# A Mamba block with an fp8 FFN: root, chunk load, tile copy and one low part moved in the first stage

## The chip, the cores and the metric

The kernel runs on 1 core of one Trainium2 chip. The metric is the device time of one execution in microseconds (us); the median of 3 runs before the change is 1058.67.

## The reference

Four sequences of 512 positions with 512 features; DI = 1024 channels, N = 16 states, 4 taps, R = 128.

```python
xn = layernorm(x)
proj = einsum('blh,eh->bel', xn, Win); hs, gate = proj[:, :DI], proj[:, DI:]
hs = silu(causal_conv4(hs) + bconv)
dt_in, Bm, Cm = split(einsum('bdl,pd->blp', hs, Wx))
dt = softplus(einsum('blr,dr->bld', dt_in, Wdt) + bdt)
h = exp(A * dt) * h + dt * Bm * hs          # scan over l, for every channel and state
y = (sum_n h * Cm + hs * D) * silu(gate)
ffn = dot8(gelu(dot8(xn, w0)) * dot8(xn, w1), w_linear)      # operands in fp8 e4m3
out = x + y @ Wout.T + ffn
```

## The kernel before

There are two stages, one after the other, written out by hand for each engine. **Stage A** (`stage_a`) makes for each of the 4 batches everything that the scan needs and leaves it in DRAM; **stage B** (`stage_b`) runs the scan, the gate, the FFN and the output projection for 32 units (4 batches by 8 channel tiles of 128). Each engine executes its instructions in the order written; semaphores tie them. On SP and TensorE the first three batches are one loop, on the others they are written out.

Stage A for batch b, with k the channel tile (8 of them), h one of the 4 feature tiles:

- TensorE (`tensor_a`) projects tile k in 12 matmuls of 512 columns (`project`; each product is split into a high and a low part of both operands, L625 to L627), and from k = 3 on adds `ssm_inputs(k - 3)` after it: five matmuls of hs_hi and hs_lo, the first, from hs_lo, written to dt_ps at L625 ("low product"). At the batch's end come low products 5, 6, 7 with the transposes of the next batch's xn between them, then eight `project_dt` (L673), one for each k, beside the four parts of the next batch's projection 0, then its projection 1.
- ScalarE (`scalar_a`): `newest_tap(b, k)` (L550) starts the convolution of tile k from PSUM, `silu` (L563) ends it, `high_part` (L568) rounds it. `deviation(b + 1)` (L525) is the square root for the next batch's layernorm; it needs a table load of its own, and one to come back (L584). `copy_tiles` (L514, L515) copies a transposed tile of the next batch out of PSUM, the fourth after the load of the table for Exp and Ln (L599). Then eight times Exp and Ln (L604, L606), with the next batch's tap 0 between units 5 and 6.
- VectorE (`vector_a`): three steps of convolution a tile (`convolve`, L445, 128x512 each), at k = 3 the layernorm's `scales` (L410 to L416), at k = 1, 4, 7 the cast of a 1 MB chunk of FFN weights to fp8 (L473), at the end the `statistics` for batch b + 2 (L399 to L405, in batches 0 and 1), then bc (L489), and for each k the sum with its cap (L483) and dt (L495).
- POOL (`gpsimd_a`): the low part hs_lo = hs - hs_hi of each tile (L362), two tiles of the next batch's xn (L367), the four low parts of its transposed tiles (L373), and dt times hs for each k (L378, "du"). In the last batch `head_start` (L858) stands before the du: the first three dbu products of stage B, 128x1024 each.
- SP (`sync_a`) issues all DMAs from one queue: the xnT store (L299), at k = 0, 3, 6 a cast chunk's store and the next chunk's load (L287, L262), a store of each hs (L307), of each dt and du together (L322, four slots: dt of tile k waits for the store of tile k - 4), and in the last batch loads for stage B (L311, L317).

```python
                if not last:
                    for h in range(HT):
                        pool.wait_ge(xnT_ready, (b + 1) * HT + h + 1 + 2)
                        nc.gpsimd.tensor_tensor(xnT_lo[:, h, :], xnT[:, h, :], xnT_hi[:, h, :], ALU.subtract).then_inc(lo_ready, 1)
```

## Time and profile before

| | us |
|---|---|
| median of 3 runs (lowest, highest) | 1058.67 (1058.31, 1058.89) |
| profiled execution, its own time | 1060.56 |
| its span | 1058.8 |
| busy: TensorE, VectorE, ScalarE, POOL | 910.5, 994.5, 832.8, 913.0 |

| stretch, us | TensorE busy | VectorE | ScalarE | POOL | granted clock | DMA share |
|---|---|---|---|---|---|---|
| 26 to 70 (batch 0) | 38.65 | 35.51 | 38.22 | 28.09 | 0.96 | 0.72 |
| 70 to 116 (batch 1) | 41.73 | 38.89 | 38.83 | 30.44 | 1.00 | 0.80 |
| 116 to 161 (batch 2) | 41.62 | 34.41 | 39.10 | 30.38 | 1.00 | 0.81 |
| 161 to 205 (batch 3) | 34.96 | 32.59 | 30.47 | 27.89 | 1.00 | 0.95 |
| 205 to 1058 (stage B) | 739.44 | 836.50 | 671.47 | 785.98 | 0.95 | 0.31 |

The page gives the span and each engine's busy time in it; the second table is the view of busy time by stretch of time. Batch boundaries are those of ScalarE's first silu table. A timeline row gives start and duration of one instruction and, in brackets, how long its engine stood idle before it and what ended that. Times of the trace lie within one execution; its own time is 1.76 us above the span, and 1.9 us above the median of the runs.

### The profile page before, as it was taken

The numbers are of one execution on the slowest core, as the hardware profiler recorded it, in microseconds if no ns is written. First come the engines' busy times: TensorE is split into PE (matmuls) and PEld (weight loads), VectorE is DVE, ScalarE is ACT, GpSimd is POOL, SyncE is SP. The second block draws the span as 40 slices with busy tenths as digits, with TensorE's granted clock in tenths as the row PEclk, the third lists the DMA queues.
The fourth block names the chain that finished last, engine by engine and source line by source line (L and its number), as shares of the span: only waits on it lengthen the run. The fifth ranks groups of instructions, "written<-read, shape, count | busy, mean of one in ns | idle before, by whom it ended". The sixth has DMA issues, their size and how long they took to land.

```text
span 1058.8 us, 14443 instructions
## 1 busy us (share of the span) xinstructions
PE 910.5 (86%) x4328; PEld 561.2 (53%) x4328; DVE 994.5 (94%) x1190; ACT 832.8 (79%) x1164; POOL 913.0 (86%) x512
## 2 busy tenths in 40 slices
PE   5888989577789987998799879887998798879998
PEld 4656757244445554554455556554555455445554
DVE  6887878799999999999999999999999999999996
ACT  5888987688888666898896668988866689888662
POOL 4566674899999899899999998999899989998993
PEclk9999999889889998999999979998999899999999
DMA  8678879991112129232121292221213922212101
GB/s 305 219 264 281 302 264 345 377 334 55 61 41 90 40 75 332 107 103 80 60 90 41 97 346 88 86 80 60 90 41 115 350 78 75 80 59 81 41 1 40
DMA packets 53208, 150.26 MB, mean 142 GB/s; under 512 B 5776, under 2 KB 14096, under 8 KB 50064
## 3 DMA queue, kind: packets, MB, share of 16 engines
q1 hardware_dynamic: 53136, 149.41, 40.6%
q8 instruction: 32, 0.52, 0.2%
q14 instruction: 40, 0.33, 0.1%
HBM read 111.37 MB, written 38.01 MB: 141 GB/s over the span
## 4 chain that ended last, share of the span: by engine, by line
DVE 32%; issue 25%; POOL 17%; ACT 11%; PE 7%; DMA 6%; SPq 1%; DVEq 1%; POOLq 0%; ACTq 0%
POOL dbu L858 11%; DVE da L1125 11%; DVE prod L1100 8%; DVE hp L1125 6%; POOL hp L1088 4%; DMA wf<-in_wffn 3%; ACT da L1019 2%; DVE conv L445 2%; PE yT L1251 2%; ACT L1008 1%; ACT L1007 1%; DVE gate_bf L1138 1%; DVE y L1108 1%; PE mm L1200 1%; DMA b_all<-bc_d 1%
## 5 line engine op out<-in xcount | busy, mean ns | idle before, releaser
L1019 ACT ACTIVATE da<-unit,neg_a 128x512 f32<-128x512 f32 x512 | 338.6, 684 | 156.9 <-DVE prod L1100 154.0
L858 POOL TENSOR_TENSOR dbu<-unit,b_head 128x1024 f32<-128x1024 f32 x192 | 450.0, 2367 | 0.0
L1125 DVE TENSOR_TENSOR_SCAN da<-da,dbu 128x512 f32<-128x512 f32 x352 | 417.9, 1218 | 1.3
L1251 PE MATMUL yT<-ident,prod 128*128 128x128 f32 x1408 | 227.7, 291 | 93.0 <-DVE prod L1100 92.2
L1251 PEld LDWEIGHTS yT<-ident,prod 128*128 128x128 f32 x1408 | 168.2, 147 | 227.7 <-DVE prod L1100 188.2
L1088 POOL TENSOR_TENSOR hp<-hp,c_head 128x512 f32<-128x512 f32 x128 | 162.7, 1271 | 50.7 <-DVE gate_bf L1141 46.1
L1125 DVE TENSOR_TENSOR_SCAN hp<-da,dbu 128x512 f32<-128x512 f32 x160 | 193.5, 1210 | 3.3 <-ACT da L1019 3.3
L1100 DVE TENSOR_TENSOR prod<-da,c_head 128x512 f32<-128x512 f32 x256 | 171.7, 671 | 0.0
L1200 PE MATMUL mm<-xn_b,w_sb 128*128 128x512 fp8e4 x512 | 143.8, 414 | 15.9 <-ACT acc L1039 12.9
L858 POOL TENSOR_TENSOR dbu<-unit,b_all 128x1024 f32<-128x1024 f32 x64 | 151.0, 2359 | 0.0
L1212 PE MATMUL mm<-xnT_b,wgate 128*128 128x512 f32 x256 | 128.8, 601 | 0.0
L1160 PE MATMUL mm<-y,wout_sb 128*128 128x512 f32 x242 | 114.6, 593 | 0.8 <-DVE y L1108 0.8
L1251 PE MATMUL yT<-ident,hp 128*128 128x128 f32 x640 | 98.9, 278 | 0.0
L1200 PEld LDWEIGHTS mm<-xn_b,w_sb 128*128 128x128 fp8e4 x512 | 51.5, 105 | 66.0 <-issue 34.7
L362 POOL TENSOR_TENSOR hs_lo<-hs,hs_hi 128x512 fp32r<-128x512 f32 x32 | 41.8, 1307 | 44.8 <-ACT hs_hi L568 44.8
L445 DVE SCALAR_TENSOR_TENSOR conv<-proj,cols_sb,conv 128x511 f32<-128x511 f32 (+2 forms) x96 | 71.0, 746 | 8.7 <-ACT conv L550 6.3
L1251 PEld LDWEIGHTS yT<-ident,hp 128*128 128x128 f32 x640 | 77.6, 145 | 0.0
L1160 PEld LDWEIGHTS mm<-y,wout_sb 128*128 128x128 f32 x242 | 43.4, 190 | 43.0 <-issue 41.9
L1100 DVE TENSOR_TENSOR prod<-da,c_all 128x512 f32<-128x512 f32 x96 | 65.0, 678 | 0.0
L1221 PE MATMUL mm<-act,w_sb 128*128 128x512 fp8e4 x256 | 61.8, 379 | 0.0
L625 PE MATMUL proj<-xnT_lo,win_hi 128*128 128x512 f32 x128 | 57.0, 446 | 0.2 <-DVE conv L445 0.2
L378 POOL TENSOR_TENSOR dt_du<-dt_du,hs 128x512 f32<-128x512 f32 x32 | 40.9, 1283 | 13.0 <-DVE dt_du L495 12.4
(123 smaller groups left out, 1285.8 us busy)
## 6 DMA issues: line engine op xcount, KB each, us to landing
unit<-unit_d SPq DMA_DIRECT2D x32, 768.0 KB, 4.2
unit_d<-dt_du SPq DMA_DIRECT2D x32, 512.0 KB, 2.9
wf<-in_wffn SPq DMA_DIRECT2D x12, 1024.0 KB, 7.1
c_head<-bc_d SPq DMA_DIRECT2D x24, 512.0 KB, 4.1
b_head<-bc_d SPq DMA_DIRECT2D x18, 512.0 KB, 4.9
unit_d<-hs SPq DMA_DIRECT2D x32, 256.0 KB, 6.6
w_sb<-w_d SPq DMA_DIRECT2D x64, 128.0 KB, 3.8
wgate<-in_win_gate SPq DMA_DIRECT2D x32, 256.0 KB, 2.7
```

The lines of the kernel that those rows point to most:

```text
L445: ins = nc.vector.scalar_tensor_tensor(out=conv[:, k % 2, back:L], in0=proj[k % 3][:, 0:L - back], scalar=cols_sb[:, k, C_TAP + TAPS - 1 - ...
L625: nc.tensor.matmul(bank, hi, low, start=start, stop=False)
L858: return nc.gpsimd.tensor_tensor(dbu[:, n % DBUS:n % DBUS + NS, :], twice, b_all[n // NS], ALU.mult)
L1019: nc.scalar.activation(da[n % SLOTS][:, :], unit[:, k % 2, 0, :], ACT.Exp, scale=neg_a[:, k, n:n + 1]).then_inc(da_ready, 1)
L1088: nc.gpsimd.tensor_tensor(tile, tile, c_all[m // NS][:, m % NS, :], ALU.mult).then_inc(hp_ready, 1)
L1100: nc.vector.tensor_tensor(prod[:, slot, :], da[n % SLOTS][:, :], c_all[n // NS][:, n % NS, :], ALU.mult).then_inc(prod_ready, 1)
L1125: nc.vector.tensor_tensor_scan(state, da[n % SLOTS][:, :], dbu[:, n % DBUS, :], 0.0, ALU.mult, ALU.add).then_inc(scanned, 1)
L1160: return nc.tensor.matmul(bank[:, :], wout_sb[:, c, h * P:(h + 1) * P], y2[:, c, :], start=(c == first), stop=(c == last))
L1200: ins = nc.tensor.matmul(bank[:, :], wffn[:, k % 2, j, f, s, :].bitcast(FP8), xn8[:, f, :].bitcast(FP8), start=(f == 0), stop=(f == HT - 1))
L1212: ins = nc.tensor.matmul(bank[:, :], wgate[:, k % 2, c * P:(c + 1) * P], xnT[:, c, :], start=(c == 0), stop=(c == 3))
L1221: ins = nc.tensor.matmul(bank[:, :], wlin[:, i, h * P:(h + 1) * P].bitcast(FP8), act8[:, i, :].bitcast(FP8), start=(i == 0), stop=(i == HI ...
L1251: ins = nc.tensor.matmul(yT[k % 2][:, t * P:(t + 1) * P], product[:, t * P:(t + 1) * P], ident[:, :], start=False, stop=last, is_transpose ...
```

## The change

Four steps, all in stage A.

- SP: the chunk's store and the next chunk's load at k = 0 are issued before the xnT store instead of after it, in every batch.
- ScalarE: the square root for the next batch moves from after two tiles to the top of the batch, behind tap 1; of the silu table's two loads in a batch one is left. In the last batch, without a root, tap 1 now stands ahead of the table load.
- ScalarE and POOL: the copy of the next batch's fourth tile moves behind the first two Exp and Ln, its low part on POOL behind the first two du.
- VectorE and POOL: in batches 2 and 3 hs_lo of k = 7 is made by VectorE, behind its last convolution and ahead of the third cast, and no longer by POOL.

```diff
--- before.py
+++ after.py
@@ -295,11 +295,12 @@
                         wait(dt_du_stored[i], 16 * (B - 1) * (KU // DTS) + 16)
                     wait(win_split, KU)
                     wait(xn_used, B)
-                wait(xnT_ready, b * HT + HT + 2)
-                sp.dma_start(row(xnT_d, b), xnT[:, :, :].rearrange("p k l -> p (k l)")).then_inc(xnT_stored, 16)
                 for k in range(KU):
                     if k % 3 == 0:
                         chunk(k // 3)
+                    if k == 0:
+                        wait(xnT_ready, b * HT + HT + 2)
+                        sp.dma_start(row(xnT_d, b), xnT[:, :, :].rearrange("p k l -> p (k l)")).then_inc(xnT_stored, 16)
                     if k == KU - 1:
                         wait(xn8_ready, b + 1)
                         sp.dma_start(row(xn8_d, b), xn8[:, :, :].rearrange("p k l -> p (k l)")).then_inc(xn8_stored, 16)
@@ -357,6 +358,8 @@
 
             def body(b, last):
                 for k in range(KU):
+                    if k == KU - 1 and b >= B - 2:
+                        continue
                     pool.wait_ge(hs_hi_ready, b * KU + k + 1)
                     pool.wait_ge(ssm_summed, b * KU + k + 1)
                     nc.gpsimd.tensor_tensor(hs_lo[:, k % 2, :], hs[:, k, :], hs_hi[:, k % 2, :], ALU.subtract).then_inc(hs_lo_ready, 1)
@@ -367,15 +370,20 @@
                             ins = nc.gpsimd.tensor_scalar(xn[:, t, :], x_rest[:, b * LT + t, :], moments[:, t, 0:1], rstd[:, t:t + 1],
                                                           ALU.subtract, ALU.mult)
                         ins.then_inc(xn_ready, 1)
+                def low_tile(h):
+                    pool.wait_ge(xnT_ready, (b + 1) * HT + h + 1 + 2)
+                    nc.gpsimd.tensor_tensor(xnT_lo[:, h, :], xnT[:, h, :], xnT_hi[:, h, :], ALU.subtract).then_inc(lo_ready, 1)
+
                 if not last:
-                    for h in range(HT):
-                        pool.wait_ge(xnT_ready, (b + 1) * HT + h + 1 + 2)
-                        nc.gpsimd.tensor_tensor(xnT_lo[:, h, :], xnT[:, h, :], xnT_hi[:, h, :], ALU.subtract).then_inc(lo_ready, 1)
+                    for h in range(HT - 1):
+                        low_tile(h)
                 if last:
                     head_start(pool)
                 for k in range(KU):
                     pool.wait_ge(dt_ready, b * KU + k + 1 + KU)
                     nc.gpsimd.tensor_tensor(dt_du[:, k % DTS, 1, :], dt_du[:, k % DTS, 0, :], hs[:, k, :], ALU.mult).then_inc(du_ready, 1)
+                    if k == 1 and not last:
+                        low_tile(HT - 1)
 
             for b in range(B):
                 body(b, b == B - 1)
@@ -462,6 +470,11 @@
                 for k in range(KU):
                     if k > 0:
                         convolve(b, k)
+                    if k == KU - 1 and b >= B - 2:
+                        dve.wait_ge(hs_hi_ready, b * KU + k + 1)
+                        dve.wait_ge(ssm_summed, b * KU + k + 1)
+                        dve.wait_ge(hs_lo_ready, b * KU + k)
+                        nc.vector.tensor_tensor(hs_lo[:, k % 2, :], hs[:, k, :], hs_hi[:, k % 2, :], ALU.subtract).then_inc(hs_lo_ready, 1)
                     if k == 3 and not last:
                         scales(b + 1)
                     if k in (1, 4, 7):
@@ -567,9 +580,13 @@
                     act.wait_ge(ssm_summed, b * KU + k + 1)
                     nc.scalar.activation(hs_hi[:, k % 2, :], hs[:, k, :], ACT.Copy).then_inc(hs_hi_ready, 1)
 
+                newest_tap(b, 1)
+                if not last:
+                    deviation(b + 1)
                 nc.scalar.preload_act_table_set("silu_and_others")
                 for k in range(1, KU):
-                    newest_tap(b, k)
+                    if k > 1:
+                        newest_tap(b, k)
                     if k == 5 and not last:
                         act.wait_ge(scales_ready, b + 2)
                         act.wait_ge(xn_used, b + 1)
@@ -579,9 +596,6 @@
                         ins.then_inc(xn_ready, 1)
                     silu(k - 1)
                     high_part(k - 1)
-                    if k == 2 and not last:
-                        deviation(b + 1)
-                        nc.scalar.preload_act_table_set("silu_and_others")
                     if k == 4:
                         fp8_copy(b)
 
@@ -597,9 +611,9 @@
                 nc.scalar.activation(dtin[:, :], dt_ps[:, :], ACT.Copy).then_inc(dtin_copied, 1)
                 nc.scalar.activation(bc_low[:, :], bc_ps[2 * N:4 * N, :], ACT.Copy).then_inc(bc_low_copied, 1)
                 nc.scalar.preload_act_table_set("natural_log_exp_and_others")
-                if not last:
-                    copy_tiles(b + 1, HT - 1, HT)
                 for k in range(KU):
+                    if k == 2 and not last:
+                        copy_tiles(b + 1, HT - 1, HT)
                     act.wait_ge(z_ready, b * KU + k + 1)
                     nc.scalar.activation(soft[:, k % 3, :], soft[:, k % 3, :], ACT.Exp).then_inc(exp_done, 1)
                     act.wait_ge(exp_done, b * KU + k + 1)
```

ScalarE at the head of batch 0, as the programs order it (sd<-vare is the root, conv<-proj a tap, hs<-conv a silu, hs_hi<-hs the copy behind it). Before:

```order
L532 ACTIVATE win_hi<-win_rest 128x512 x2
L570 ACT_TABLE_LOAD
L550 ACTIVATE conv<-proj,cols_sb 128x512
L563 ACTIVATE hs<-conv 128x512
L568 ACTIVATE hs_hi<-hs 128x512
L550 ACTIVATE conv<-proj,cols_sb 128x512
L563 ACTIVATE hs<-conv 128x512
L568 ACTIVATE hs_hi<-hs 128x512
L525 ACT_TABLE_LOAD
L525 ACTIVATE sd<-vare 128x4
L584 ACT_TABLE_LOAD
L550 ACTIVATE conv<-proj,cols_sb 128x512
```

And of the change:

```order
L545 ACTIVATE win_hi<-win_rest 128x512 x2
L563 ACTIVATE conv<-proj,cols_sb 128x512
L538 ACT_TABLE_LOAD
L538 ACTIVATE sd<-vare 128x4
L586 ACT_TABLE_LOAD
L576 ACTIVATE hs<-conv 128x512
L581 ACTIVATE hs_hi<-hs 128x512
L563 ACTIVATE conv<-proj,cols_sb 128x512
L576 ACTIVATE hs<-conv 128x512
L581 ACTIVATE hs_hi<-hs 128x512
```

One table load is gone, and the first silu stands behind the root and two loads instead of behind one load and a tap.

SP at the start of batch 3 (xnT_d is the 1 MB store, w_d the cast chunk's store, wf the next chunk's load). Before:

```order
L299 DMA xnT_d<-xnT 128x2048
L287 DMA w_d<-w 128x2048
L262 DMA wf<-in_wffn 128x2048
L307 DMA unit_d<-hs 128x512
L317 DMA unit<-unit_d 128x1536
```

And of the change:

```order
L287 DMA w_d<-w 128x2048
L262 DMA wf<-in_wffn 128x2048
L303 DMA xnT_d<-xnT 128x2048
L308 DMA unit_d<-hs 128x512
L318 DMA unit<-unit_d 128x1536
```

The load has only the chunk's own store ahead of it in the batch.

POOL from batch 2's second half to the du of batch 3 (hs_lo are the low parts, unit<-c_head xn, dbu the head start). Before:

```order
L362 TENSOR_TENSOR hs_lo<-hs,hs_hi 128x512 x4
L373 TENSOR_TENSOR xnT_lo<-xnT,xnT_hi 128x512 x4
L378 TENSOR_TENSOR dt_du<-dt_du,hs 128x512 x8
L362 TENSOR_TENSOR hs_lo<-hs,hs_hi 128x512 x8
L858 TENSOR_TENSOR dbu<-unit,b_head 128x1024 x3
```

And of the change:

```order
L365 TENSOR_TENSOR hs_lo<-hs,hs_hi 128x512 x3
L375 TENSOR_TENSOR xnT_lo<-xnT,xnT_hi 128x512 x3
L384 TENSOR_TENSOR dt_du<-dt_du,hs 128x512 x2
L375 TENSOR_TENSOR xnT_lo<-xnT,xnT_hi 128x512
L384 TENSOR_TENSOR dt_du<-dt_du,hs 128x512 x6
L365 TENSOR_TENSOR hs_lo<-hs,hs_hi 128x512 x7
L872 TENSOR_TENSOR dbu<-unit,b_head 128x1024 x3
```

POOL makes seven low parts in batch 3 before the head start instead of eight, and the fourth tile's low part stands between du 1 and du 2.

## Rows read from the trace of the kernel before

**Rows 1.** timeline of PE, tails of batches 0 to 3: start, duration, instruction [idle before]
```profile
47.49 0.39 PE L625 MATMUL dt_ps<-hs_lo,wx_hi 128*128 128x512 f32 x1
...
53.56 0.50 PE L625 MATMUL dt_ps<-hs_lo,wx_hi 128*128 128x512 f32 x1 [0.63 <-POOL hs_lo L362]
...
92.25 0.39 PE L625 MATMUL dt_ps<-hs_lo,wx_hi 128*128 128x512 f32 x1
...
99.67 0.50 PE L625 MATMUL dt_ps<-hs_lo,wx_hi 128*128 128x512 f32 x1 [0.77 <-POOL hs_lo L362]
...
137.19 0.39 PE L625 MATMUL dt_ps<-hs_lo,wx_hi 128*128 128x512 f32 x1
...
144.34 0.49 PE L625 MATMUL dt_ps<-hs_lo,wx_hi 128*128 128x512 f32 x1 [0.55 <-POOL hs_lo L362]
...
181.90 0.39 PE L625 MATMUL dt_ps<-hs_lo,wx_hi 128*128 128x512 f32 x1
...
188.70 0.50 PE L625 MATMUL dt_ps<-hs_lo,wx_hi 128*128 128x512 f32 x1 [0.80 <-POOL hs_lo L362]
```

**Rows 2.** VectorE's second cast in batch 3, and the landing of all chunk loads
```profile
178.06 1.23 DVE L473 TENSOR_SCALAR w<-wf 128x2048 fp8e4<-128x2048 f32 x1 [4.35 <-DMA wf<-in_wffn]
...
DMA to landing us min/median/max: 6.3/7.1/10.4
```

**Rows 3.** timeline of POOL and DVE in batch 3: head start, first and fifth dt_du
```profile
188.61 7.96 POOL L858 TENSOR_TENSOR dbu<-unit,b_head 128x1024 f32<-128x1024 f32 x3
...
194.09 0.75 DVE L495 SCALAR_TENSOR_TENSOR dt_du<-z_ps,cols_sb,soft 128x512 f32<-128x512 f32 x1 [0.52 <-ACT soft L606]
...
201.27 0.75 DVE L495 SCALAR_TENSOR_TENSOR dt_du<-dt_ps,cols_sb,soft 128x512 f32<-128x512 f32 x1 [1.68 <-DMA unit_d<-dt_du]
```

**Rows 4.** timelines of ACT, DVE and PE at the head of batch 0; a window of clock
```profile
27.39 0.62 ACT L563 ACTIVATE hs<-conv 128x512 f32<-128x512 f32 x1
...
31.18 1.28 ACT L525 ACT_TABLE_LOAD   x1
...
32.70 1.28 ACT L584 ACT_TABLE_LOAD   x1
...
27.23 0.17 DVE L405 TENSOR_SCALAR vare<-moments 128x4 f32<-128x4 f32 x1
...
30.27 0.47 PE L625 MATMUL dt_ps<-hs_lo,wx_hi 128*128 128x512 f32 x1 [2.80 <-POOL hs_lo L362]
...
31.10:34.30 3.20, 3.20 (x9) 2.38 (x8) 2.15 (x3) 3.14 (x5) 1.29 (x1) 0.50 0.67 172
```

**Rows 5.** ACT before the first softplus of batch 0, and its waits from 58 to 70
```profile
57.55 0.60 ACT L514 ACTIVATE xnT_hi<-tp 128x512 fp32r<-128x512 f32 x1
...
58.52 0.63 ACT L604 ACTIVATE soft<-soft 128x512 f32<-128x512 f32 x1
...
ACT soft L604 <- DVE soft L483: 0.8, 3, 0.3
```

**Rows 6.** chain of waits, 60 to 72: start, duration, what
```profile
64.96 5.06 DMA unit_d<-dt_du
```

**Rows 7.** timeline of PE: last z product, projection 2, first low product
```profile
66.40 1.12 PE L673 MATMUL dt_ps<-dtin,wdt_sb 128*128 128x512 f32 x2
...
70.11 0.39 PE L625 MATMUL proj<-xnT_lo,win_hi 128*128 128x512 f32 x1
...
76.62 0.47 PE L625 MATMUL dt_ps<-hs_lo,wx_hi 128*128 128x512 f32 x1 [0.47 <-POOL hs_lo L362]
...
112.50 0.70 PE L673 MATMUL dt_ps<-dtin,wdt_sb 128*128 128x512 f32 x1
...
121.64 0.40 PE L625 MATMUL dt_ps<-hs_lo,wx_hi 128*128 128x512 f32 x1
```

**Rows 8.** timelines of POOL and DVE in the tail of batch 0
```profile
53.46 3.75 POOL L373 TENSOR_TENSOR xnT_lo<-xnT,xnT_hi 128x512 fp32r<-128x512 f32 x3
...
55.04 0.97 DVE L405 TENSOR_SCALAR vare<-moments 128x4 f32<-128x4 f32 x1
```

## The prediction

> **What bounds the kernel now.** I read the busy time by stage first (the table by stretches), then in stage A the waits and the timelines of each engine; stage B only at its first instructions. Stage A is the first 205 us. Stage B after it is one long chain on VectorE, and nothing in it is edited, so it should begin earlier or later as a whole and keep its length.
>
> In stage A no engine is the limit throughout. TensorE runs without a gap from the first low product of a batch (hs_lo of k=0) to that of k=4, and then waits three times for hs_lo. The reader should see how long the tail from k=4 to k=7 is in each batch [rows 1]: 53.56-47.49 = 6.1 us in batch 0, but 7.4, 7.2 and 6.8 in batches 1, 2 and 3. The excess of 1.35, 1.1 and 0.7 us is VectorE's: its second weight cast stood waiting for the chunk's load, 4.35 us in batch 3 [rows 2], and three convolutions are queued behind it. After the tail come dtin, a table load, eight softplus units, and in the last batch POOL's head start: three dbu products from 188.61 to 188.61+7.96 = 196.57, and only then the first du [rows 3]. The store of that du frees the slot that the fifth dt_du needs, so VectorE idles 1.68 us until 201.27 [rows 3]. That wait ends last in stage A.
>
> **The change, part by part.** All times are starts; a plus is later than before.
>
> *Root in batch 0.* Now the first silu starts at 27.39, and the square root's two table loads stand at 31.18 and 32.70, after two units [rows 4]. Moved to the top, the root waits for the variance: vare ends at 27.23+0.17 = 27.40 [rows 4]. Then root and table load: from 31.18 to 32.70 is 1.52 us, of which 1.28 the first load, so 0.24 for the root, then 1.28+0.02 for the second. The first silu starts at 27.42+0.24+1.30 = 28.96, **+1.6**. From that silu to TensorE's first low product it is 30.27-27.39 = 2.88 [rows 4]; the product starts at 31.84. TensorE has no slack behind it in this batch, so 1.6 stays. Its clock stood at 0.50 for 3.2 us after the present idle [rows 4], that is 1.2 GHz. A longer idle can lengthen or shift this; at half speed 1 us of slow time costs 0.5, so I keep ±0.5 for it.
>
> The removed table load (three, one a batch) is worth 1.28 us of ScalarE each. The Trainium skill, "ScalarE: Activation LUTs", section "What ACT_TABLE_LOAD costs", adds a drain of about 1.38 us to every switch. By it each removed load would be worth 2.66 us, and an estimate by that page would take off up to 4.1 us more over three batches. The trace does not agree: the load at 31.18 ends at 32.46 and the second begins at 32.70, 0.24 on, with the root's own activation between them [rows 4]. So it gets no chance below.
>
> *Fourth tile behind two softplus.* The two copies start at 57.55, when the table is in, and the first Exp at 58.52 [rows 5]; it could start about 0.9 earlier. The copies' 0.97 us are not saved, only moved. What can vanish is ScalarE's idle time in the softplus, 0.8 us in three waits [rows 5]. Bounds are 0 and 0.8 (0.9 if TensorE's z products, which wait for the first dt_du, gain it all); I take **-0.5** for batches 0, 1 and 2. POOL's low part of that tile goes between du 1 and du 2 and is done before TensorE's fourth part asks for it; du 2 and its store come 1.3 us later relative to du 0. That matters in batch 0, where this store took 5.06 us and dt_du 6 waited for it [rows 6].
>
> *Root in batch 1.* The last z product starts at 66.40 now, so at 66.40+1.6-0.5 = 67.5. Tile 1's newest tap now stands ahead of both loads and must wait for TensorE's projection 1, which ends 70.11-66.40 = 3.71 behind that product [rows 7]. Add 0.2 to reach ScalarE and 0.7 for the tap (estimates; a silu takes 0.62 [rows 4]), 2.8 for load, root and load as above, and 2.88 to the first low product: 67.5+10.3 = 77.8, against 76.62 [rows 7]: **+1.2**. If dt_du 6 again waits 5 us for its store, +1.7; if not at all and the softplus gives 0.9, +0.8.
>
> *Chunk's load ahead of the store.* The xnT store of 1 MB no longer stands before the chunk's load on SP's queue. In batch 3 the wait was 4.35 us, and from issue to landing a chunk took between 6.3 and 10.4 us [rows 2]. I take it that near the lower end is what a load without that megabyte ahead needs; that is 4 us sooner, enough to end the wait, and the excess of the tails goes. Batch 1's last low product: 92.25+1.2+6.07 = 99.5 against 99.67 [rows 1], **-0.15**: the earlier load only pays for the late root. The xnT store gets later and is asked for only when the next batch's first tile is copied, in the tail; the hs stores behind it are asked for a batch later. Both cost nothing.
>
> *Batch 2.* Last z product 112.50-0.15-0.5 = 111.85, first low product 10.3 later at 122.15, against 121.64 [rows 7]: **+0.5**. Tail: 137.19+0.5+6.07 = 143.8. Here VectorE makes the last low part. A subtraction of this size takes POOL 1.25 (3.75 for three) [rows 8], and I estimate 0.7 on VectorE, from its 128x512 dt_du of 0.75 [rows 3]. So 143.3 against 144.34: **-1.0**. No statistics stand behind it on VectorE in batches 2 and 3, only a cast; the sum for bc behind that waits for ScalarE's bc_low, which comes later. Cost nothing; without that cover the cast's delay of 2 us would show.
>
> *Batch 3.* There is no root. With -1.0-0.5 from before, TensorE runs through, and the low product of k=4 starts at 180.4 instead of 181.90 [rows 1]. POOL, rid of its last low part, finishes low part 6 about 3.5 later (0.2 to reach ScalarE, tap 0.7, silu 0.65, copy 0.65, low part 1.3) and begins the head start at 184.0 instead of 188.61 [rows 3]. VectorE's low part is ready to run a tail less POOL's 1.3 after the k=4 product, 6.07-1.3 = 4.8, at 185.2, in the middle of the first dbu product. That is a conflict that the trace of before shows elsewhere: the 4-element vare, 0.17 us long elsewhere [rows 4], took VectorE 0.97 us from 55.04, ending at 56.01, just as POOL's second of three subtractions ended (53.46+2x1.25 = 55.96) [rows 8]. I take it that VectorE waits until the dbu product ends at 186.4, so the last low product starts at 187.15 against 188.70: **-1.55**, and the dbu products shift by 0.7. The rule behind it is in the Trainium skill, "SBUF — State Buffer", section "SBUF: two separate sides": VectorE with two SBUF inputs and GpSimd take their shared port pair exclusively, and whoever starts second is blocked for the whole instruction; the trace agrees with it as far as that row goes.
>
> The first du then starts at 193.35 (first dt_du 194.09-1.55 [rows 3], plus 0.8; the three dbu end at 184.0+7.96+0.7 = 192.7 and no longer hold it) instead of 196.57 [rows 3]: -3.2. Its store, issued some 1.3 later, frees the slot after another 3.4, at 198.05 (now from 196.57 to 201.27, 4.7 in all); the softplus chain itself, whose idle time before the fifth dt_du was 1.68, arrives at 201.27-1.68-1.55 = 198.05, too. So the fifth dt_du moves from 201.27 to 198.1, **-3.2**, and with it the start of stage B; I book -3.1.
>
> **Sum: -3.1 us.** The running total is +1.6 after batch 0, -0.15 after batch 1, -1.0 after batch 2, -1.55 at the last low product of batch 3, and -3.1 once du 0 no longer waits for POOL. The profiled execution took 1060.56 (span 1058.8), so 1057.5 for its like; against the median of 1058.67 it gives 1055.6. A measurement of this kernel can tell about 0.2%, 2.1 us, from no change.
>
> **The rivals.**
> 1. *No conflict on VectorE's low part.* For it: the two may miss each other, since both starts are known to 1 us only. Against it: POOL is busy there for 8 us on end [rows 3], and the row of 0.97 us [rows 8]. The last low product would start at 185.9, du 0 at 192.1, all -4.3: **1054.4**.
> 2. *The last batch's gain goes to the DMA queue.* The du stores then come among the c_head loads. For it: one such store took 5.06 [rows 6], where about 3.4 are in the sum. Against it: these loads are issued earlier, too. If du 0's store takes 5.1, the fifth dt_du starts 1.7 later, -1.4: **1057.3**.
> 3. *Slower.* The root's place costs 1.6 in batch 0, and the load, though ahead, lands no earlier since load and store share the DMA engines. Then the second cast stays the limit in batches 1 to 3, shifted by 1.6 with nothing won. It decides if the second cast of batch 3 still waits over 4 us. Batch 3 gives back 0.8 of it by POOL; with 0.5 of clock, nothing from the softplus and dt_du 6 of batch 0 waiting 1.2 more for its store: +2.5, **1061.2**. Against it: the fastest chunk took 6.3 us against 10.4 for the slowest [rows 2], so something ahead in the queue does count.
>
> **How the numbers follow.** Chances: forecast 0.58, rival 1 0.17, rival 2 0.17, rival 3 0.08. Of the forecast's own spread (±0.5 clock, 0.4 to 0.5 each for batch 1's root and the softplus) some 0.07 falls short of 2.1 us. Faster 0.51+0.17 = 0.68; within 0.2% 0.07+0.17+0.01 = 0.25; slower 0.07. The range 1053.6 to 1058.2 reaches from rival 1 with 0.8 to spare to rival 2 with 0.8.
>
> **What would show it.** In the profile after: batch 0's first silu near 28.9 and its first low product near 31.8; a new TensorE wait of about 1 us before the first low product in batches 1 and 2; second casts that hardly wait for their chunk; tails of about 6.1 us in batch 1 and 5.6 in batch 2; VectorE's low part in batch 3 over 1.5 us long or late; the first dbu near 184, the first du near 193.4, stage B's first scan at 203.0 instead of 206.07. It is wrong if the casts still wait, if the clock stays low much beyond 35 us, or if stage B changes its length.

## The result, and the profile after

| | kernel before | changed kernel |
|---|---|---|
| median of its runs, us | 1058.78 (8 runs, 1058.01 to 1061.25) | 1063.76 (8 runs, 1061.81 to 1064.54) |
| ratio, 95% interval | | 1.0040 (1.0029 to 1.0051) |
| profiled execution, own time / span, us | 1060.56 / 1058.8 | 1062.02 / 1060.2 |
| its mean granted clock | 0.956 | 0.952 |

The changed kernel is slower by 0.4%: 4.2 us, 3.1 to 5.4 by the interval. The forecast was 3.1 us faster. One warning belongs ahead of all rows: the profiled execution of before lies 1.8 us above its median and that of the changed kernel 1.7 us below its own. The two traces differ by 1.5 us, the medians by 5.0. So the traces tell where time went, and sizes are taken from timed runs or from several traces.

Stage B kept its length: from its first scan to the end it is 1058.8-206.07 = 852.7 us before and 1060.2-207.69 = 852.5 after, and 852.5 to 853.1 in each trace of this study. All of it is in stage A.

Head of batch 0, timelines of ScalarE, POOL and TensorE of the changed kernel (start, duration, instruction, idle before), answering to [rows 4]:

```profile
27.41 0.20 ACT L538 ACTIVATE sd<-vare 128x4 f32<-128x4 f32 x1 [0.69 <-DVE vare L413]
27.63 1.28 ACT L586 ACT_TABLE_LOAD   x1
28.92 0.63 ACT L576 ACTIVATE hs<-conv 128x512 f32<-128x512 f32 x1
...
30.29 1.56 POOL L365 TENSOR_TENSOR hs_lo<-hs,hs_hi 128x512 fp32r<-128x512 f32 x1 [3.62 <-ACT hs_hi L581]
...
32.11 0.77 PE L639 MATMUL dt_ps<-hs_lo,wx_hi 128*128 128x512 f32 x1 [4.84 <-POOL hs_lo L365]
32.67 0.63 PE L640 MATMUL dt_ps<-hs_hi,wx_lo 128*128 128x512 f32 x1
33.10 0.63 PE L641 MATMUL dt_ps<-hs_hi,wx_hi 128*128 128x512 f32 x1
...
38.79 0.39 PE L639 MATMUL dt_ps<-hs_lo,wx_hi 128*128 128x512 f32 x1
39.01 0.39 PE L640 MATMUL dt_ps<-hs_hi,wx_lo 128*128 128x512 f32 x1
39.24 0.40 PE L641 MATMUL dt_ps<-hs_hi,wx_hi 128*128 128x512 f32 x1
```

And two windows of TensorE there (length, busy us of PE, PEld, DVE, ACT, POOL, then the granted clock, DMA share, GB/s):

```profile
32.10:38.10 6.00, 5.99 (x15) 4.49 (x16) 5.10 (x11) 1.90 (x3) 2.56 (x2) 0.51 0.97 277
38.10:46.00 7.90, 7.90 (x36) 6.27 (x35) 5.78 (x7) 6.82 (x9) 4.97 (x3) 1.00 0.70 228
```

The root and the silu stand where the forecast put them (28.96 expected, 28.92 found). POOL's first low part takes 1.56 us, beside VectorE's first cast (29.51 to 30.73), where it took 1.27 before, so the first low product comes at 32.11 instead of 31.84. And TensorE idles 4.84 us, and then runs at 0.51 of full speed (1.2 GHz) for 6 us, not for 3.2. Matmuls start 0.43 us apart there and 0.23 us apart behind it. The second low product is 6.68 us behind the first, 5.56 before; 38.79 is 2.96 us later than before, where +1.6 was booked.

The tails, TensorE, answering to [rows 1]:

```profile
50.45 0.39 PE L639 MATMUL dt_ps<-hs_lo,wx_hi 128*128 128x512 f32 x1
...
95.04 0.39 PE L639 MATMUL dt_ps<-hs_lo,wx_hi 128*128 128x512 f32 x1
...
139.93 0.39 PE L639 MATMUL dt_ps<-hs_lo,wx_hi 128*128 128x512 f32 x1
...
182.55 0.39 PE L639 MATMUL dt_ps<-hs_lo,wx_hi 128*128 128x512 f32 x1
...
188.99 0.80 PE L639 MATMUL dt_ps<-hs_lo,wx_hi 128*128 128x512 f32 x1 [1.46 <-DVE hs_lo L477]
```

The last low products of batches 0 to 2 start at 56.52, 101.11 and 145.37, so the tails are 6.07, 6.07 and 5.44 us as forecast (6.1 and 5.6 for batches 1 and 2). The batch is shorter, but it begins late. At the last low product of batch 3 the changed kernel is still 0.3 us behind.

Batch 3, VectorE and POOL, answering to [rows 2, 3]:

```profile
175.21 1.23 DVE L486 TENSOR_SCALAR w<-wf 128x2048 fp8e4<-128x2048 f32 x1 [0.91 <-DMA wf<-in_wffn]
...
187.25 1.69 DVE L477 TENSOR_TENSOR hs_lo<-hs,hs_hi 128x512 fp32r<-128x512 f32 x1 [1.36 <-ACT hs_hi L581]
188.86 3.38 DVE L486 TENSOR_SCALAR w<-wf 128x2048 fp8e4<-128x2048 f32 x1
...
196.67 0.74 DVE L508 SCALAR_TENSOR_TENSOR dt_du<-z_ps,cols_sb,soft 128x512 f32<-128x512 f32 x1
...
202.94 0.75 DVE L508 SCALAR_TENSOR_TENSOR dt_du<-dt_ps,cols_sb,soft 128x512 f32<-128x512 f32 x1 [0.36 <-DMA unit_d<-dt_du]
...
186.01 8.43 POOL L872 TENSOR_TENSOR dbu<-unit,b_head 128x1024 f32<-128x1024 f32 x3
```

The second cast waits 0.91 us for its chunk instead of 4.35, and POOL's head start begins 2.6 us earlier. VectorE's low part takes 1.69 us beside the dbu products, where the one in batch 2, with no dbu product beside it, takes 0.69. The third cast behind it takes 3.38 us; it took 1.53 before. Then the fifth dt_du is 202.94-188.99 = 13.95 us behind the last low product; it was 12.57 before, and 10.95 was forecast. The wait for a du store is only 0.36 us of it here. What stretched it in this trace is TensorE, at half its clock from the last low product on (windows as above; before had 1.00 in both):

```profile
192.18 2.08 PE L687 MATMUL z_ps<-dtin,wdt_sb 128*128 128x512 f32 x2 [0.69 <-ACT dtin L611]
...
189.00:192.00 3.00, 2.50 (x5) 1.27 (x5) 3.00 (x1) 0.47 (x1) 3.00 (x2) 0.50 1.05 419
192.00:195.00 3.00, 2.82 (x4) 1.27 (x5) 1.63 (x3) 2.00 (x3) 2.44 (x1) 0.50 0.71 267
```

Two z products take 2.08 us, and the first dt_du comes 7.68 us behind the last low product; it was 5.39 before.

### The profile page after: what moved, and what is told of

The parts are those of the page before. It is cut to its first block, busy times and chain, and to the rows that moved or that the text cites. A ratio compares the mean times of both kernels' runs of the same rounds, so it can differ in the third digit from the quotient of the medians.

```text
span 1060.2 us, 14430 instructions
## 1 busy us (share of the span) xinstructions
PE 915.8 (86%) x4318; PEld 563.4 (53%) x4328; DVE 1001.2 (94%) x1192; ACT 828.5 (78%) x1161; POOL 913.9 (86%) x510
## 4 chain that ended last, share of the span: by engine, by line
DVE 42%; issue 22%; PE 18%; ACT 12%; POOL 2%; DMA 2%; DVEq 1%; SPq 0%; POOLq 0%; ACTq 0%
DVE da L1139 17%; DVE prod L1114 11%; DVE hp L1139 9%; PE yT L1265 3%; ACT da L1033 3%; PE mm L1174 2%; PE mm L1214 2%; DVE y L1122 2%; PE proj L640 2%; PE proj L641 2%; PE proj L639 2%; ACT L1022 1%; ACT L1021 1%; PE mm L1226 1%; DVE gate_bf L1152 1%
```

## The experiments

The kernels ran in groups of four, one group for each section below, each group on one chip beside runs of the kernel before; ratios are to those. The parts of the change stand behind constants in them:

```
ROOT_TOP     batches with the root at the top of the body
LOW_DVE      batches in which VectorE makes the last low part
COPY_LATE    batches with the fourth tile behind two softplus units
CHUNK_FIRST  a chunk's load ahead of the xnT store
```

The changed kernel is (0, 1, 2), (2, 3), (0, 1, 2), True; the kernel before is (), (), (), False. With a root at the top of any batch, tap 1 of batch 3 stands ahead of the table load, too, as in the changed kernel.

| run | ROOT_TOP, LOW_DVE, COPY_LATE, CHUNK_FIRST | else | ratio (95%) |
|---|---|---|---|
| root_only | 0-2, -, -, no | | 1.0045 (1.0032 to 1.0059) |
| chunk_only | -, -, -, yes | | 0.9986 (0.9975 to 0.9996) |
| copy_only | -, -, 0-2, no | | 0.9980 (0.9971 to 0.9988) |
| low_only | -, 2-3, -, no | | 1.0004 (0.9994 to 1.0014) |
| root0_only | 0, -, -, no | | 1.0033 (1.0022 to 1.0045) |
| no_root0 | 1-2, 2-3, 0-2, yes | | 1.0011 (1.0000 to 1.0022) |
| no_root | -, 2-3, 0-2, yes | | 0.9982 (0.9973 to 0.9991) |
| no_root_low3 | -, 2, 0-2, yes | | 0.9966 (0.9953 to 0.9979) |
| full_again | as changed | | 1.0034 (1.0021 to 1.0047) |
| full_fill | as changed | 16 filler matmuls | 1.0008 (0.9999 to 1.0017) |
| no_low3 | 0-2, 2, 0-2, yes | | 1.0011 (1.0003 to 1.0020) |
| best_fill | as no_root_low3 | 8 filler matmuls | 0.9966 (0.9953 to 0.9979) |
| full_store | as changed | third store later | 1.0017 (1.0008 to 1.0027) |
| full_noport | as changed | head start later | 1.0025 (1.0016 to 1.0034) |
| best_store | as best_fill | third store later | 0.9939 (0.9926 to 0.9953) |
| best_store3 | as best_store, LOW_DVE 2-3 | | 0.9941 (0.9928 to 0.9955) |

0.001 is 1.06 us. An interval is some 1.1 us to either side, so a difference of two runs is known to about 1.5 us.

### Each part alone

```
root_only:  +ROOT_TOP = (0, 1, 2)
chunk_only: +CHUNK_FIRST = True
copy_only:  +COPY_LATE = (0, 1, 2)
low_only:   +LOW_DVE = (2, 3)
```

> The kernel before with the root's step alone (tap 1, root, silu table at the top of every batch). Theory A, cold clock: TensorE's idle before batch 0's first low product grows from 2.8 to 4.8 us, its clock then stays at 0.50 for some 6 us instead of 3, and the tail of batch 0 ends 3 us late; batches 1 and 2 start their first low product 10.4 us behind the last z product instead of 10.2 and 9.1, part of which the late chunk load hides. Time +2.5 us (1.5 to 4). Rival B, the step is harmless and the loss lies in the other steps: the table load saved gives -1 to 0. Rival C, stage B is what became slower: under 0.5 us either way in stage A.

> The kernel before with the chunk's load ahead of the xnT store alone. Theory A: the second cast's waits of 1.67, 2.02 and 4.35 us in batches 1 to 3 vanish or fall below 1 us, the tails of these batches shrink from 7.4, 7.2 and 6.8 to about 6.1 us, and the time falls by 3 us (2 to 3.5). Rival B: the load lands sooner but something else (hs stores, unit loads of batch 3) comes late, and the time is within 1 us of before.

> The kernel before with the fourth tile's copy and low part behind two softplus units alone. Theory A: each of batches 0 to 2 shortens by 0.4 us at the last z product, and the late chunk load leaves at most 0.4 to 1.2 us of it in the time: -0.8. Rival B, the copies in the middle and the later du stores cost more than the earlier start gives: +0.5 to +1.5.

> The kernel before with VectorE's last low part in batches 2 and 3 alone. Theory A: in batch 2 the last low product comes 0.6 us sooner; in batch 3 VectorE's low part is blocked by the first dbu product (over 1.5 us long instead of 0.7), its cast by the second (over 3 us instead of 1.3), the last low product is 0.5 to 1 us late, and TensorE's longer idle halves its clock in the z products, which costs about 2 us more: +1 us (0 to 3). Rival B: POOL's earlier head start frees the first du and its store, and with no loss on TensorE the time falls by 1.5 to 2.5 us.

Measured: root +4.8 us, above the 1.5 to 4 expected; chunk -1.5, half of the 3 expected; copy -2.1, more than the 0.8; low part +0.4, in its range. The sum, +1.6, is less than the change's +4.2 (or +3.6 in full_again), though four intervals of some 1.1 us leave little of that gap certain. Two parts are gains, and the root alone is worth the whole loss. The chunk's load ended the waits of the second casts, but in chunk_only the tails of batches 1 and 2 are 6.75 us and not 6.1: in batch 1 the third cast waits 1.00 us for its chunk, and POOL's last low part then runs beside it and takes 1.95 us instead of 1.28. low_only shows the same blocked work as the changed kernel, with its root where it was:

```profile
185.64 1.99 DVE L483 TENSOR_TENSOR hs_lo<-hs,hs_hi 128x512 fp32r<-128x512 f32 x1 [1.36 <-ACT hs_hi L587]
...
187.55 3.40 DVE L492 TENSOR_SCALAR w<-wf 128x2048 fp8e4<-128x2048 f32 x1
```

### Which root costs

```
root0_only:   root_only with ROOT_TOP = (0,)
no_root0:     changed kernel with ROOT_TOP = (1, 2)
no_root:      changed kernel with ROOT_TOP = ()
no_root_low3: no_root with LOW_DVE = (2,)
```

> The kernel before with the root at the top of the body in batch 0 alone. The root in all three batches cost +4.8 us (ratio 1.0045). Theory A (the first batch carries it: TensorE idles 1.8 to 2.0 us longer before the first low product and its slow stretch behind that gets longer; batch 1 and 2 have an idle time there anyway): +3 us (2.2 to 4), low7 of batch 0 at about 56.4, and the same +2.9 kept until batch 3, first scan near 209. Theory B (the roots of batches 1 and 2, which let TensorE idle before the first low product, where it did not before): +1 us or less, low7 of batch 0 near 55 and first scan near 207.

> The changed kernel with batch 0's root put back behind two silus; all else as changed. Theory A: the changed kernel less 3 us or more, so about 1.5 us faster than the kernel before (ratio 0.998 to 0.999). Theory B (roots of batches 1 and 2 carry the cost): +2 to +4 against the kernel before (ratio 1.002 to 1.004).

> The changed kernel with the root back behind two silus in all batches: the chunk's load ahead (alone -1.5), the late fourth tile (alone -2.0) and VectorE's low part (alone 0 to +1) remain. If the parts add up: -2.5 to -3.5 us (ratio 0.997). Rival: the last batch gives the gains back by its slow TensorE clock, or VectorE's low part and POOL's dbu block one another: 0 to -1 us. Its trace should show VectorE's low part of batch 3 taking over 1.5 us beside a dbu.

> As the one before, and VectorE makes the last low part in batch 2 alone; in batch 3 POOL makes it, so POOL's head start stands behind it and cannot block VectorE. Theory: the low part in batch 3 costs what it gains, so this is the same as the run before or up to 1 us faster: -3 to -4 us against the kernel before (ratio 0.9965). Rival: the earlier head start was worth its 2 us, and this one is 1 to 2 us slower than the run before; then the first du again starts behind three dbu products, with VectorE idle over 1.5 us before the fifth dt_du.

Batch 0's root alone costs 3.5 us of root_only's 4.8. Taken out of the changed kernel it gives back 1.0040-1.0011, 3.1 us (2.4 against full_again). The roots of batches 1 and 2 are the other part: no_root is 3.1 us faster than no_root0, though root_only less root0_only gives only 1.3. So in the changed kernel batch 0's root and the other two cost about the same. Theory A was right for root0_only and wrong for no_root0, which is no faster than the kernel before. In the traces of no_root and no_root0 the first low product of a batch starts 22.2 against 23.7 us behind the last one of the batch before in batch 1, and 21.6 against 23.2 in batch 2: 1.4 and 1.6 us for the two roots. The late start of those batches is seen in all traces with a root at the top; in the changed kernel, ScalarE in batch 1:

```profile
72.91 0.78 ACT L563 ACTIVATE conv<-proj,cols_sb 128x512 f32<-128x512 f32 x1 [0.41 <-PE proj L641]
73.70 1.28 ACT L538 ACT_TABLE_LOAD   x1
75.00 0.20 ACT L538 ACTIVATE sd<-vare 128x4 f32<-128x4 f32 x1
75.22 1.28 ACT L586 ACT_TABLE_LOAD   x1
76.52 0.63 ACT L576 ACTIVATE hs<-conv 128x512 f32<-128x512 f32 x1
```

The last z product is at 68.98 and the first low product at 79.41, 10.43 behind it; it was 10.22 before. In batch 2 that distance is 10.72 against 9.14. With no root at the top all gains together are worth -1.9 us with VectorE's low part in batch 3 and -3.6 without it, so that low part costs 1.7 us there; 0 to 1 was expected.

### Filling TensorE's idle time

```
full_fill, TensorE's program, batch 0 only, ahead of ssm_inputs(0):
+for i in range(16):
+    nc.tensor.matmul(dt_ps[:, :], win_hi[:, 0, 0:P], xnT_hi[:, 0, :], start=True, stop=True)
best_fill: no_root_low3 with range(8)
```

All kernels with fillers also have TensorE's first batch written out instead of run as the first pass of the loop. No kernel has that alone, so its effect isn't separated from the fillers'.

> The changed kernel once more, instruction for instruction, beside the runs below on one chip. +4 to +5 us against the kernel before. If batch 0's root carries about 3.3 of it (alone it cost 3.5) and part of that is TensorE's slow stretch behind the longer idle time, this trace too shows the first low product of batch 0 near 32, then matmuls at 0.43 us spacing instead of 0.23 for over 5 us.

> The changed kernel with 16 throwaway matmuls (products of xnT's and win's high parts into dt_ps, which the first low product overwrites) that TensorE runs in batch 0 while it waits for hs_lo of k=0; for that, TensorE's program is unrolled for batch 0. They take 16 x 0.23 = 3.7 us of 4.8 us of idle time and delay nothing. Theory (the slow clock behind the idle time is half of what batch 0's root costs): clock 1.00 behind the first low product, which stays near 32; the second low product follows 3.9 us later instead of 6.7; low7 of batch 0 near 53.7 instead of 56.5, and 2 to 3 us less than the changed kernel. Rival (the clock falls whatever fills the gap, or the time is lost elsewhere): same as the changed kernel within 0.7 us.

> The changed kernel (roots at the top), but POOL makes the last low part of batch 3, so its head start does not run beside VectorE's low part and cast. Theory: that low part gives back what it wins, so this is up to 1.5 us faster than the changed kernel: +3 to +4.5 against the kernel before. Rival: it is worth over 1 us, and this is +5.5 to +6.5. Its trace should show the third cast of batch 3 at 1.2 to 1.5 us instead of 3.4, and the clock at 1.00 between 189 and 192.

> The fastest version so far (chunk's load ahead, late fourth tile, VectorE's low part in batch 2 alone, root where it was: -3.6 us) with 8 throwaway matmuls before the first low product of batch 0. They take 1.8 us of 2.1 to 2.8 us of idle time. Theory: the slow stretch of batch 0, where it occurs (in 5 of the 7 traces with the root where it was), costs 1.4 to 2.8 us; 1 us less on average, so -4 to -5.5 against the kernel before. Rival: no more than -3.6, since that stretch is mostly absent or the later waits absorb it.

full_again came out at +3.6 us, its first low product at 32.01, the second 5.84 behind. full_fill, whose fillers are overwritten by the first low product, shows the clock at 1.00 through the same work. TensorE's timeline:

```profile
26.93 3.79 PE L707 MATMUL dt_ps<-xnT_hi,win_hi 128*128 128x512 f32 x16
33.22 0.50 PE L652 MATMUL dt_ps<-hs_lo,wx_hi 128*128 128x512 f32 x1 [2.50 <-POOL hs_lo L369]
```

and by windows:

```profile
33.20:37.20 4.00, 3.98 (x17) 3.19 (x18) 3.86 (x7) 2.10 (x4) 2.55 (x2) 1.00 0.96 250
```

An idle time of 2.50 us is left and the clock does not fall; the second low product follows after 4.00 us. The kernel is 2.8 us faster than full_again (3.4 than the changed kernel's first measurement). So the slow clock very likely carries a part of the loss; by the trace that is 5.84-4.00 = 1.8 us of the distance. The first low product was 1.2 us later here than in full_again: a small VectorE instruction ahead of the statistics, 128x128, took 1.39 us from 24.17 beside POOL's subtractions, 0.21 in full_again, and vare came 1.4 us later, 1.2 of it by this. So at the last low product of batch 0 this trace is only 0.6 us ahead.

Over all traces, the head of batch 0:

| | traces | idle before first low product, us | its start, mean | distance to the second, us (mean) |
|---|---|---|---|---|
| root after two units | 7 | 1.46 to 3.14 | 29.9 | 3.97 to 6.75 (5.3) |
| root at the top | 7 | 4.57 to 5.32 | 32.1 | 5.49 to 6.70 (6.0) |
| with fillers | 4 | | | 3.89 to 4.61 |

So the root at the top makes the first low product 2.2 us later and the clock adds 0.7 on average: 2.9 in all, against 3.5 (2.3 to 4.7) in root0_only. (In the distance also lie waits for VectorE of some 0.65 us, in two traces of the first row.) Not all of the 0.7 lasts: where TensorE runs at full clock it waits for VectorE soon after, and the last low product of batch 0 starts at 53.3 in the mean of the first row and at 55.9 in that of the second, 2.6 us later. With the short idle time the slow stretch is missing in three of seven traces, one more than best_fill's expectation counted; with the long one it is there in all seven, for 3.3 to 6 us of work. best_fill measured -3.6 by ratio, no more than no_root_low3; its medians (1054.98 and 1056.17) leave room for 1 us, so whether fillers help there stays open. The traces of best_fill, best_store and best_store3 reach the first low product of batch 1 in 21.6 us from the last of batch 0, where no_root and no_root_low3 take 22.2 and 22.5; no filler stands there, so some of what these kernels win may be the written-out batch or chance.

no_low3 is 2.4 us faster than full_again, more than the 1.5 expected at most: with roots at the top, too, the low part on VectorE in batch 3 loses time. Its third cast takes 1.75 us and its head start begins at 188.15. The clock, though, is at 0.72 from 189 to 192, not at 1.00 as expected, so the clock there isn't VectorE's doing alone.

### The last stretch of batch 3

This is where the forecast's -1.6 between the last low product and the fifth dt_du should have come from. The order on SP's queue is the store of the third cast (w_d), hs 6, a c_head load, xn8, hs 7, a c_head load, bc, and then the du stores. The timeline of SP's queue before:

```profile
189.82 0.33 SPq L287 DMA_DIRECT2D w_d<-w  x1
190.26 0.37 SPq L307 DMA_DIRECT2D unit_d<-hs  x1
190.68 0.51 SPq L311 DMA_DIRECT2D c_head<-bc_d  x1
...
197.89 7.24 SPq L322 DMA_DIRECT2D unit_d<-dt_du  x6
```

and in full_again:

```profile
191.43 0.33 SPq L288 DMA_DIRECT2D w_d<-w  x1
191.87 1.23 SPq L312 DMA_DIRECT2D unit_d<-hs  x1
193.15 0.43 SPq L316 DMA_DIRECT2D c_head<-bc_d  x1
193.68 0.39 SPq L310 DMA_DIRECT2D xn_d<-xn  x1
194.19 0.37 SPq L312 DMA_DIRECT2D unit_d<-hs  x1
194.60 0.49 SPq L316 DMA_DIRECT2D c_head<-bc_d  x1
195.20 0.71 SPq L324 DMA_DIRECT2D bc_d<-bc  x1
196.14 8.77 SPq L327 DMA_DIRECT2D unit_d<-dt_du  x5
```

The cast ends at 187.94+3.40 = 191.34 and the whole queue stands behind it. The du stores come right on the loads (two c_head loads; the expectations below say four). The chain of waits has the store of the first du, before and in full_again (start, duration):

```profile
197.89 3.28 DMA unit_d<-dt_du
```

```profile
196.14 6.15 DMA unit_d<-dt_du
```

It was issued 1.75 us earlier and landed 1.1 us later. VectorE's rows in full_again, with the clock at 1.00:

```profile
193.94 0.75 DVE L514 SCALAR_TENSOR_TENSOR dt_du<-z_ps,cols_sb,soft 128x512 f32<-128x512 f32 x1 [0.70 <-ACT soft L633]
...
202.38 0.75 DVE L514 SCALAR_TENSOR_TENSOR dt_du<-dt_ps,cols_sb,soft 128x512 f32<-128x512 f32 x1 [2.00 <-DMA unit_d<-dt_du]
...
189.00:192.00 3.00, 2.31 (x8) 0.70 (x6) 3.00 (x3) 2.44 (x3) 3.00 (x2) 1.00 1.01 405
```

The first dt_du is 5.88 us behind the last low product here, against 7.68 in the changed kernel's first trace, and the fifth waits 2.00 us for its slot, against 0.36. So two executions of the same instructions lose the same 14 us in two ways: one by TensorE's clock, the other by the du store. Two kernels test the queue and the blocked VectorE:

```
full_store, SP, last batch only: (and best_store, best_store3)
-                    if k % 3 == 0:
+                    if k % 3 == 0 and not (last and k == 6):
                         chunk(k // 3)
...
                 sp.dma_start(row(bc_d, b), bc[:, :]).then_inc(bc_stored, 16)
+                if last:
+                    chunk(2)
full_noport, POOL, ahead of the head start:
+                    pool.wait_ge(w8_ready, CHUNKS)
best_store3: best_store with LOW_DVE = (2, 3)
```

> The changed kernel; in the last batch alone the store of VectorE's third cast moves on SP's queue from ahead of hs 6 to behind bc's store. VectorE and POOL block one another as before (cast 3.4 us). Theory (the blocked cast holds SP's queue, so that hs 6, hs 7 and four c_head loads are issued at 192 to 195 instead of near 186 to 191 and land on the du stores): this store no longer holds them, du 0's store takes about 3.5 us instead of 6, and the time falls by 1.5 to 2.5 us against the changed kernel. Rival (VectorE's own delay or the clock lengthens the last stretch): within 0.7 us of the changed kernel; fifth dt_du still over 13.3 us behind the last low product.

> The changed kernel, and POOL begins its head start only when VectorE's third cast of batch 3 is done, so no low part and no cast runs beside a dbu. VectorE's low part 0.7 us, the cast 1.2 to 1.6, the last low product 0.9 earlier than in the changed kernel, w's store on SP's queue near 188; the dbu products start near 188 and the first du again waits for them (near 196). Theory (what the port conflict costs is the whole of the lengthening): fifth dt_du near 200.5, 1.5 to 2.5 us less than the changed kernel, like no_low3. Rival (the low part on VectorE costs otherwise): no gain.

> The fastest version (root where it was, chunk first, late fourth tile, VectorE's low part in batch 2, 8 throwaway matmuls) with the store of the third cast behind bc's store. The cast is hardly late here (1.2 to 1.8 us, 2.8 in one trace), so 0 to -0.7 us against that version: -3.5 to -5 against the kernel before.

> As the one before, with VectorE's low part in batch 3 too. If SP's queue was what took the gain of the early head start, this is the fastest: 1 to 2 us less than best_store, -5 to -6.5 against the kernel before. Rival (the blocked VectorE or the du stores still cost it): no faster than best_store.

In full_store the low part (1.69 us) and the cast (3.40 us) are blocked as before, but SP goes on without them, and the fifth dt_du has no DMA wait. TensorE's clock was as in full_again, 1.00 for eight us behind the last low product and 0.50 for some three after that:

```profile
187.72 3.40 DVE L494 TENSOR_SCALAR w<-wf 128x2048 fp8e4<-128x2048 f32 x1
...
185.88 0.50 SPq L316 DMA_DIRECT2D c_head<-bc_d  x1
191.80 0.34 SPq L324 DMA_DIRECT2D bc_d<-bc  x1
192.25 0.68 SPq L288 DMA_DIRECT2D w_d<-w  x1
...
200.23 0.74 DVE L516 SCALAR_TENSOR_TENSOR dt_du<-dt_ps,cols_sb,soft 128x512 f32<-128x512 f32 x1
```

The stretch from the last low product to the fifth dt_du, over all traces, with TensorE's granted clock in the eight us behind that product:

| last low part by | third store | clock there | traces | us |
|---|---|---|---|---|
| VectorE, beside dbu | waits for the blocked cast | 1.00 | 2 (full_again, full_fill) | 14.3, 13.3 |
| VectorE, beside dbu | waits for the blocked cast | 0.50 for 3 to 8 us | 4 | 13.9 to 14.7 |
| VectorE, beside dbu | moved | 1.00 | 2 (full_store, best_store3) | 12.4, 12.1 |
| VectorE, dbu behind the cast (full_noport) | not held | 0.50 for 6 us | 1 | 13.3 |
| POOL | cast 1.23 to 1.75 us | 1.00, two at 0.50 for 3 us | 7 | 12.3 to 12.8 |
| POOL, cast 2.78 us (best_fill, ends at 184.0) | held | 1.00 | 1 | 14.0 |
| POOL, cast 2.88 us (best_store) | moved | 1.00 | 1 | 12.5 |

Two pairs differ in the store's place alone: full_again to full_store, 14.3 to 12.4, and best_fill to best_store, 14.0 to 12.5. Moving one store on SP's queue so shortens the stretch by 1.5 to 1.9 us in the traces, and the kernel by 1.8 us (full_again to full_store; 2.4 from the first measurement; the two ran on different chips). best_store over best_fill wins 2.9 by ratio and 1.7 by medians, more than expected of it. full_noport removes the conflict (low part 0.69, cast 1.23, the last low product 5.44 us behind that of k=4 instead of 6.45), but gives 1.0 us against full_again and 1.6 against the first measurement, at or below the lower end of the 1.5 to 2.5 expected: dbu starts at 189.3, and TensorE ran at 0.50 from 189 to 195 in this trace. So the queue is shown to carry most of the lengthening where the clock is full. Where the clock falls right behind the last low product, as in the changed kernel's first trace, the clock does: the first dt_du is then 7.4 to 7.7 us behind (three traces) instead of 5.9. How often either happens in the timed runs is open, and so is VectorE's own share. best_store3 equals best_store within some 1.5 us, where 1 to 2 us less was expected: once the queue is free, no cost and no gain of the low part on VectorE is seen.

**The fastest version** is best_store: root where it was, the chunk's load ahead, the late fourth tile, VectorE's low part in batch 2 alone, 8 fillers, the third store of the last batch behind bc's. 1053.29 us (5 runs, 1052.96 to 1054.16), ratio 0.9939 (0.9926 to 0.9953), 6.5 us faster than the kernel before, and faster than the changed kernel by about 10. best_store3 is its equal within the noise.

## Why the prediction was wrong, point by point

Where the trace of the changed kernel left the forecast:

| start of | forecast | trace | late by, us |
|---|---|---|---|
| last low product of batch 0 | 55.2 | 56.52 | 1.4 |
| last low product of batch 2 | 143.3 | 145.37 | 2.1 |
| last low product of batch 3 | 187.15 | 188.99 | 1.8 |
| fifth dt_du of batch 3 | 198.1 | 202.94 | 4.8 |

So two steps failed: the last stretch of batch 3, by 3.0 us, and the root in batch 0, by 1.4 us in the trace and by 1 to 2 in the means and timed runs.

- **Root in batch 0, +1.6 ± 0.5: failed.** The silu was right to 0.05 us, the first low product 0.3 late by POOL's longer low part. Two more things were not right. The trace of before is above average at this place: its idle time of 2.80 us [rows 4] is the second longest of seven, and against their mean the root costs 2.2 us, not 1.6. And the clock was booked as noise of either sign. In single traces it is that (6.75 us of distance in chunk_only, 5.49 in full_store), but not in the mean: +0.7 to the second low product, +1.1 in this trace. Together 2.6 us at the batch's end by the means and 3.5 in root0_only instead of 1.6.
- **Roots of batches 1 and 2, 10.3 us behind the last z product:** nearly right (10.4 and 10.7). The sum let the chunk's load and the softplus pay for them. They did, but had batch 0's loss to pay too: at the last low product of batch 1 the trace is +1.4 instead of -0.15, of batch 2 +1.0 instead of -1.0. That these roots were not free shows in no_root, 3.1 us faster than no_root0.
- **No drain of 1.38 us with a table load:** right; the load at 27.63 takes 1.28 us and the silu starts at 28.92, which leaves no room for one. The Trainium skill, "ScalarE: Activation LUTs", section "What ACT_TABLE_LOAD costs", has that drain with every switch and would have made the removed loads worth more; the runs with the root at the top are the slower ones.
- **Softplus, -0.5:** measured by copy_only at -2.1 for three batches, the size forecast (-1.5) within its interval. The traces put the earlier softplus itself at 0.4 us a batch: from the last low product to the last z product it is 13.0 us with the late tile and 13.4 without it.
- **Chunk's load ahead:** right. Waits of 4.35 us fell to 0.9, the tails of the changed kernel are 6.07 us; chunk_only gives -1.5 us. Rival 3's premise (the load lands no sooner) is refuted. Its sign came true by another way.
- **VectorE's low part blocked by dbu:** right in kind and size: 1.69 us, against 1.9 (185.2 until 187.1) forecast. The Trainium skill, "SBUF — State Buffer", section "SBUF: two separate sides", has VectorE with two SBUF inputs and GpSimd exclude one another on a shared port pair, and this row agrees. The cast behind it was held as well and took 3.4 us instead of 1.5. The prediction named such a delay, took it as covered by the wait of bc's sum for bc_low, and booked nothing. The cover was 0.6 us short: in full_again ScalarE has bc_low ready at 190.14+0.59 = 190.73 and the cast ends at 191.34. That an instruction reading one tensor is held, too, stood in its own rows: the vare of 0.97 us [rows 8] reads one, like the cast.
- **From the last low product to the fifth dt_du, 10.95 us: the step that failed most.** It took 13.95, and 14.31 in full_again. Behind the cast stood SP's queue with its c_head loads, which the prediction did not follow, and the sums for bc and the first z, for which it saw enough cover (the first dt_du is 0.5 late even in full_store, 5.88 us behind the last low product instead of 5.39). Beside these there is TensorE's clock, for which the sum has no term here: 0.50 for the nine us behind the last low product in the first trace, 0.66 in 195 to 200 in both traces of the changed kernel, 1.00 before. Rival 2 had the effect, the du store among the c_head loads, at 5.1 us; it was 6.15 in full_again. It was given 0.17 because "these loads are issued earlier, too". They are issued later, since w's store stands ahead of them.
- **Stage B's length:** unchanged, right.

What no run settles is why two traces differ by 1.5 us and the medians by 5: the single traces of the changed kernel show +1.6 and +2.0 at the first scan, its timed runs 3.6 and 4.2. The trace of before lies above its median and that of the changed kernel below, but where in stage A that spread sits would need several traces of each.

## What to carry to other kernels

An instruction moved ahead of what TensorE waits for costs its own length and what the longer idle time does to TensorE's clock; here the second part was a loss in the mean of seven traces, and the kernel with throwaway matmuls ahead of it (and a written-out batch) was 2.8 us faster. When an instruction is put on an engine where another one may block it, cost every instruction behind it as blocked, and follow each queue that waits for them to its end: here one late cast held a store, the store held the loads, and the loads ran into the transfers that ended the stage. A single trace has a place in its kernel's spread: before rows of it are taken as the base, look whether its own time is above or below the median, and take a second one before a wait in it is called the cause.

## What was not expected of the hardware

- Throwaway matmuls that leave 2.5 us of idle time kept the clock at 1.00 (full_fill), where 2.80 us without them, in the kernel before, and 2.64 in no_root did not. In no_root_low3 and low_only idle times of 2.08 and 2.40 us left the clock at 1.00, while 1.82 us in no_root0 ended in a slow stretch (0.61 and 0.54 in the two windows from 30 to 34). So the idle time before it alone does not decide.
- A cast of 128x2048 on VectorE takes 1.22 us alone and 3.34 to 3.40 beside POOL's 128x1024 products (seven traces; 3.15 in best_store3, and 2.78 and 2.88 in best_fill and best_store, where POOL's products start just ahead of it), 2.2 longer, where one product takes 7.96/3 = 2.65 [rows 3]. In batch 1 of the changed kernel, beside POOL's first low part, one took 2.29.
- With one 256 KB store in another place on SP's queue, later 512 KB stores took 3.0 us in the median from 190 to 206 (full_store) instead of 5.9 (full_again). The place alone doesn't decide it: in the changed kernel's first trace, with the order of full_again but the first of these stores issued 2.7 us later, they took 3.4.
- Two executions of the same instructions (the changed kernel and full_again) had TensorE's clock at 0.50 and at 1.00 through the same eight us behind the last low product, 188.99 and 188.07.
